# Channel mix moved to a matrix product, x by key read from a host-laid copy, three-slot pipeline

## The chip, the cores and the metric

One Trainium2 chip, one of its cores. The metric is the device time of one execution in microseconds (us), lower is better. Engines are named as in the profile: PE is TensorE (matmuls; PEld its weight loads), ACT is ScalarE, DVE is VectorE, POOL is GpSimd, and SP is SyncE, which issues the DMAs.

## The reference

x is 16 images of 256 channels and 64 x 32 pixels, float32 throughout. For each image (n is the pixel index, N = 2048):

```
alpha = relu(bn(wa @ x))           # 32 x N, queries
sigma = relu(bn(ws @ x))           # 32 x N, keys
att   = softmax over m of alpha[:, n] . sigma[:, m], only the 8 neighbours m of pixel n
h_s   = att @ x                    # spatial mix
Gc    = x x^T                      # 256 x 256, only channels c-1 and c+1 are used
catt  = softmax of Gc over the two neighbouring channels
h_p   = catt @ x                   # channel mix: two weights for each channel
out   = (1 - gama) * x + gama * elu(h_s + h_p)
```

## The kernel before

**Layout.** x of an image lies as 128 partitions by 2 halves: partition p holds channels 2p (h = 0) and 2p + 1 (h = 1), so that one neighbour of a channel is in the same partition and the other in a partition beside it. An image is cut into 4 quarters of 16 rows, 512 pixels. One quarter is a step s, 64 steps in all. Pixels are also cut into 16 groups of 128 keys; a query tile of 64 pixels needs a window of 128 keys.

**What a step computes.** `scores` (PE) writes masked windows of query by key to a bank of PSUM, two steps in one call (steps s and s + 1, for even s). `maxima` (DVE) adds the mask and takes the row maxima, `exp_scores` (ACT) exponentiates with row sums, `normalise` (DVE) divides and writes `probs`, `transpose_probs` (PE) turns it, `move_probs` copies it from PSUM to `probs_t`, and `z_sums` (PE) accumulates the spatial mix into the two banks z of the step, in two phases of 9 matmuls (`phase` 0 and 1, z_half between them). For the product PE needs x with keys on the partitions: that is `upper`, made by `transpose_x` (PE, 4 transposes of 128 x 128, two calls a step) and `move_xt` (ACT).

**The channel mix.** `weigh_own` (ACT) first writes 1 + catt * (the neighbour in the same partition) to z. `build_near` (SP) copies the other half of x one partition up or down into `near`, four DMAs a step, SBUF to SBUF. `mix_channels` (DVE) adds catt * near to z. Only then does `z_sums` accumulate on top. `exp_z` (ACT), `elu_out` (DVE), `keep_x` and `add_elu` (POOL) make the elu and the blend, and SP stores the result.

**Per image.** The projections `project_query`, `project_odd` (with two transposes of the image's last 64 keys, L525) and `project_even` fill a shared bank `gb` in turn, each waiting until ACT has emptied it (`move_query`, `move_odd`, `move_even`). `gram_band` (PE, 68 matmuls in four parts) makes the diagonals of Gc from `upper`; `gram_pick`, `shift_gram`, `gram_softmax_in`, `exp_gram` and `gram_softmax_out` turn them into `catt`.

**Order.** Each engine runs a loop over slots t, written by hand. In slot t the kernel works on scores and softmax of step t, on the transpose and the channel mix of step t - 1, on `z_sums` of step t - 2, on exp, elu and store of step t - 3, and on the transposes of x one image ahead. q is t modulo 4; the per-image work hangs on q. Engines meet only through counting semaphores. x has three buffers (XBUFS), `upper` and `near` two, `blend` four, z two pairs of banks, and the one bank `tr` takes both the turned x and the turned probabilities. Matmuls of float32 appear in the trace as two instructions each; transposes as one.

Nearly all matmuls are issued by the helper `mm`, so they have line 485, and the tiles written tell them apart: z from probs_t is `z_sums`, gb from x is a projection, gb from upper is the gram, score is the scores. Line 500 is `transpose_x`, line 581 `transpose_probs`.

## Time and profile before

| | us |
|---|---|
| median of 3 runs | 462.85 |
| lowest, highest | 458.08, 465.39 |
| the profiled execution | 457.33 |
| its span, first to last instruction | 455.5 |
| PE busy | 422.3 (93%) |
| DVE busy | 351.2 (77%) |
| ACT busy | 339.0 (74%) |
| POOL busy | 295.4 (65%) |
| DMA moved | 102.05 MB, mean 224 GB/s |

The profile describes the profiled execution alone. Its span leaves out 1.8 us that lie around the first and the last instruction. The span has three stretches: a start to about 38 us, in which the first image comes in and the pipeline fills; a repeating pattern of one image; and an end from about 424 us, in which the last image has no successor to prepare.

### The profile page before, as it was taken

To read this page: it belongs to the slowest core of one execution; us is meant where nothing else is said; L and a number is where in the kernel's file an instruction comes from. 1 tells how busy PE (TensorE), PEld (TensorE's weight loads), DVE (VectorE), ACT (ScalarE), POOL (GpSimd) and SP (SyncE) were. 2 spreads that over 40 slices of the span, in tenths; PEclk is the share of its full clock that TensorE was granted. 3 is DMA by queue.
4 is the path that set the end of the run, shared out by engine and by line. 5 is a ranking of instruction groups with operands and counts; after the bars stand their busy time and mean duration, and the time that the engine had idled before them with its cause. 6 is when DMAs were issued, how large, how long until landed. Compare 5 with 4: busy or idle time off the path is not lost.

```text
span 455.5 us, 18204 instructions
## 1 busy us (share of the span) xinstructions
PE 422.3 (93%) x7118; PEld 319.3 (70%) x7120; DVE 351.2 (77%) x1138; ACT 339.0 (74%) x980; POOL 295.4 (65%) x198
## 2 busy tenths in 40 slices
PE   6859999999999999999999989998999999999783
PEld 3426867677686777778676767877677786867673
DVE  1145878878887897888789778877978788888976
ACT  5447788686877978686888868687887868878651
POOL 5301676578588676858676676777667676787760
PEclk9959999999999999999999999999999999999776
DMA  7695678587777868777787877778687777855223
GB/s 223 187 250 155 200 253 250 195 264 229 234 246 243 265 224 264 243 229 234 246 270 222 250 232 228 243 239 268 190 263 246 228 251 237 257 183 191 96 85 148
DMA packets 55750, 102.05 MB, mean 224 GB/s; under 512 B 6256, under 2 KB 6640, under 8 KB 55664
## 3 DMA queue, kind: packets, MB, share of 16 engines
q1 hardware_dynamic: 55376, 100.81, 70.8%
q8 instruction: 57, 0.93, 0.9%
q14 instruction: 29, 0.24, 0.2%
q10 hardware_dynamic: 288, 0.07, 0.1%
HBM read 34.00 MB, written 33.55 MB: 148 GB/s over the span
## 4 chain that ended last, share of the span: by engine, by line
PE 71%; DVE 18%; issue 3%; DMA 3%; ACT 2%; SPq 1%; DVEq 0%; ACTq 0%
PE z L485 23%; PE gb L485 20%; PE tr L500 13%; PE score L485 7%; PE tr L581 6%; DVE elu L403 4%; DMA x<-x_dram 3%; DVE score L374 3%; DVE probs_t L391 2%; DVE probs L383 2%; PE gb L525 1%; DVE gb L418 1%; DVE band L414 1%; DVE neg_max L374 1%; DVE row_inv L379 1%
## 5 line engine op out<-in xcount | busy, mean ns | idle before, releaser
L485 PE MATMUL z<-probs_t,upper 64*128 64x128 f32 (+1 forms) x2304 | 173.7, 285 | 2.3 <-DVE z L398 1.2
L485 PEld LDWEIGHTS z<-probs_t,upper 64*128 64x128 f32 x2304 | 155.7, 191 | 22.0 <-issue 20.7
L239 POOL TENSOR_TENSOR blend<-elu,blend 128x1024 f32<-128x1024 f32 x61 | 144.1, 2363 | 9.4 <-POOL elu L235 0.5
L229 POOL TENSOR_SCALAR blend<-x,mix 128x1024 f32<-128x1024 f32 x64 | 71.8, 1123 | 98.8 <-DMA out_dram<-blend 98.7
L403 DVE SCALAR_TENSOR_TENSOR elu<-elu,z 128x512 f32<-128x512 f32 x128 | 82.1, 683 | 38.0 <-ACT elu L311 38.0
L288 ACT ACTIVATE score<-score,neg_max 128x128 f32<-128x128 f32 x256 | 86.7, 339 | 28.0 <-DVE neg_max L374 28.0
L311 ACT ACTIVATE elu<-z 128x512 f32<-128x512 f32 x128 | 69.7, 604 | 41.1 <-PE z L485 41.1
L261 ACT ACTIVATE upper<-tr 128x512 f32<-128x512 f32 x122 | 73.2, 600 | 34.7 <-PE tr L500 33.8
L235 POOL TENSOR_SCALAR elu<-elu,vec,mix 128x1024 f32<-128x1024 f32 x61 | 72.6, 1190 | 34.7 <-DVE elu L403 34.7
L398 DVE SCALAR_TENSOR_TENSOR z<-near,catt,z 128x512 f32<-128x512 f32 x128 | 89.9, 748 | 0.0
L500 PE MATMUL tr<-const,x 128*128 128x128 f32 x488 | 78.2, 283 | 11.4 <-DVE probs_t L391 7.2
L302 ACT ACTIVATE z<-x,catt 128x512 f32<-128x512 f32 x128 | 83.9, 697 | 2.3 <-DVE elu L403 2.3
L374 DVE CUSTOM_DVE_ANT_0 score<-score,const 128x128 f32<-128x128 f32 x256 | 66.7, 323 | 24.3 <-PE score L485 24.3
L500 PEld LDWEIGHTS tr<-const,x 128*128 128x128 f32 x488 | 53.4, 143 | 39.1 <-issue 34.3
L485 PE MATMUL gb<-x,wt 128*32 128x512 f32 (+2 forms) x720 | 65.7, 483 | 2.6 <-DMA x<-x_dram 2.6
L288 ACT ACTIVATION_READ_ACCUMULATOR score<-score,neg_max 128x1 f32 x256 | 53.1, 207 | 0.0
L383 DVE TENSOR_TENSOR probs<-score,row_inv 128x512 f32<-128x512 f32 x64 | 44.3, 692 | 2.2
L581 PE MATMUL tr<-const,probs 128*128 128x128 f32 x256 | 42.9, 291 | 2.7 <-DVE probs L383 1.9
L391 DVE COPY probs_t<-tr 128x512 f32<-128x512 f32 x64 | 44.0, 687 | 0.9 <-PE tr L581 0.9
L485 PE MATMUL score<-key,query 32*64 32x128 f32 x1024 | 36.2, 279 | 3.1 <-DVE probs L383 2.4
L485 PEld LDWEIGHTS gb<-x,wt 128*32 128x32 f32 x720 | 19.0, 110 | 25.4 <-issue 12.0
L374 DVE DVE_READ_ACCUMULATOR2_ANT neg_max<- 128x1 f32 x256 | 36.3, 142 | 0.0
(64 smaller groups left out, 254.1 us busy)
## 6 DMA issues: line engine op xcount, KB each, us to landing
x<-x_dram SPq DMA_DIRECT2D x64, 512.0 KB, 5.5
out_dram<-blend SPq DMA_DIRECT2D x61, 512.0 KB, 4.3
near<-x SPq DMA_DIRECT2D x128, 224.0 KB, 4.4
near<-x SPq DMA_DIRECT2D x128, 30.0 KB, 4.0
out_dram<-blend SPq DMA_DIRECT2D x6, 256.0 KB, 2.0
const<-constants_dram SPq DMA_DIRECT2D x1, 243.5 KB, 8.0
const<-constants_dram SPq DMA_DIRECT2D x1, 128.0 KB, 2.2
wt<-w_dram ACTq DMA_DIRECT2D x1, 64.0 KB, 2.8
```

What stands on the lines that cost most here:

```text
L229: nc.gpsimd.tensor_scalar(blend[s % BLENDS][:, :, :], xs[b % XBUFS][:, :, cols(q)], mix[:, 0:1], 0.0 if s < TAIL else mix[:, 1:2], ALU.mul ...
L235: nc.gpsimd.tensor_scalar(elu[s % 2][:, :, :], elu[s % 2][:, :, :], vec[:, V_GAMA:V_GAMA + 1], mix[:, 1:2], ALU.mult, ALU.add).then_inc(ga ...
L239: nc.gpsimd.tensor_tensor(blend[s % BLENDS][:, :, :], elu[s % 2][:, :, :], blend[s % BLENDS][:, :, :], ALU.add).then_inc(blend_done, 1)
L261: nc.scalar.activation(upper[b % 2][:, g:g + 2, :], xt_bank(b, q, i)[:, :].rearrange("p (v c) -> p v c", v=2), ACT.Copy).then_inc(xt_out, 1)
L288: last = nc.scalar.activation(at, at, ACT.Exp, bias=neg_max[s % 2][:, v:v + 1], scale=-1.0, accum_out=row_sum[s % 2][:, v:v + 1])
L302: nc.scalar.activation(z[s % 2][h][:, :], xs[b % XBUFS][:, 1 - h, cols(q)], ACT.Identity, scale=catt[:, h, 1 - h:2 - h], bias=1.0).then_in ...
L374: last = nc.vector.tensor_tensor_reduce(at, at, mask, -1.0, TOP, ALU.add, ALU.min, neg_max[s % 2][:, v:v + 1])
L398: nc.vector.scalar_tensor_tensor(zh[:, :], near[b % 2][:, h, q * QN:(q + 1) * QN], catt[:, h, h:h + 1], zh[:, :], ALU.mult, ALU.add).then_ ...
L403: nc.vector.scalar_tensor_tensor(elu[s % 2][:, h, :], elu[s % 2][:, h, :], 1.0, z[s % 2][h][:, :], ALU.min, ALU.max).then_inc(elu_done, 1)
L485: return nc.tensor.matmul(o, l, r, start=start, stop=stop, skip_group_check=True, **kw)
L500: last = nc.tensor.transpose(to[:, v * C + h * P:v * C + (h + 1) * P], xb[:, h, at0:at0 + WIN], ident)
L581: last = nc.tensor.transpose(tr[:, v * P:(v + 1) * P], probs[s % 2][:, v, :], ident)
```

## The change

- A second copy of x comes from the host, laid out by key: `x_t`, 16 x 128 x 17 x 256. SP loads it straight to `upper` (`load_upper`, two DMAs an image). `transpose_x`, `move_xt`, the two edge transposes of `project_odd` and their copy are gone. `upper` has three buffers.
- `near`, `build_near` and its four DMAs a step are gone. The channel mix is a matrix product: `build_diag` (DVE, four instructions an image) makes two 128 x 128 matrices with catt on two diagonals, `turn_diag` (PE) transposes them, `move_mixer` (ACT) copies them to `mixer`, and `mix_channels` (now on PE) multiplies them with x, two matmuls of 128 x 128 by 512 a step, accumulating to z.
- `weigh_own` becomes `set_one` (ACT): it writes 1 to z. `mix_channels` of DVE is gone. `move_probs` moves from DVE to ACT.
- The pipeline has three slots instead of four: in slot t, `transpose_probs`, `mix_channels`, both phases of `z_sums`, `exp_z` and `elu_out` all belong to step t - 1, and the store to t - 2. `gram_band` runs in one piece, an image ahead, and catt is ready an image ahead.
- `scores` of the next two steps stand at the end of the odd slots.

The loops that set the order, on PE, ACT and DVE, and the new helpers:

```
-            for t in range(STEPS + 3):
+            for t in range(STEPS + 1):
                 b, q = t // QUARTERS, t % QUARTERS
-                if b + 1 < B:
-                    transpose_x(b + 1, q, 0)
...
+                ahead = b + 1 < B
+                if real(t - 1):
                     transpose_probs(t - 1)
+                    mix_channels(t - 1)
+                if q == 1 and ahead:
+                    shift_gram(b + 1)
+                if q == 2 and ahead:
+                    project_query(b + 1)
+                if q == 3 and ahead:
+                    project_even(b + 1)
+                if real(t - 1):
+                    z_sums(t - 1, 0)
+                    z_sums(t - 1, 1)
+                if q == 0 and b < B:
+                    turn_diag(b)
+                if q == 0 and ahead:
+                    gram_band(b + 1)
+                if q == 2 and ahead:
                     project_odd(b + 1)
+                if q % 2 == 1 and t + 1 < STEPS:
+                    scores(t + 1)
```

```
+            def mix_channels(s):
+                b, q = s // QUARTERS, s % QUARTERS
+                pe.wait_ge(mixer_out, b + 1)
+                for h in range(HALF):
+                    pe.wait_ge(one_done, 2 * s + h + 1)
+                    mm(z[s % 2][h][:, :], mixer[:, h * P:(h + 1) * P], xs[b % XBUFS][:, 1 - h, cols(q)], False, True)
...
             def project_even(b):
                 xb = xs[b % XBUFS]
                 if b > 0:
-                    pe.wait_ge(odd_out, 2 * (b + 1))
+                    pe.wait_ge(odd_out, b + 1)
...
+            def turn_diag(b):
+                pe.wait_ge(diag_done, b + 1)
+                if b > 0:
+                    pe.wait_ge(pt_out, b * QUARTERS)
+                for h in range(HALF):
+                    last = nc.tensor.transpose(tr[:, h * P:(h + 1) * P], diag[:, h, :], ident)
+                last.then_inc(mixer_done, 1)
```

ACT, the new slot:

```
+                if real(t - 1):
+                    move_probs(t - 1)
+                for h in range(HALF):
+                    if real(t):
+                        set_one(t, h)
+                if q == 3 and ahead:
+                    move_odd(b + 1)
+                if real(t):
+                    exp_scores(t)
+                if q == 1 and ahead:
+                    exp_gram(b + 1)
+                if q == 2 and ahead:
                     move_query(b + 1)
+                if q == 3 and ahead:
+                    move_even(b + 1)
                 for h in range(HALF):
                     if real(t - 1):
+                        exp_z(t - 1, h)
+                if q == 0 and b < B:
+                    move_mixer(b)
```

DVE, the new slot:

```
+                if q == 1 and ahead:
+                    gram_pick(b + 1)
                 if real(t):
                     maxima(t)
+                if q == 1 and ahead:
+                    gram_softmax_in(b + 1)
+                if real(t):
                     normalise(t)
+                if q == 1 and ahead:
+                    gram_softmax_out(b + 1)
+                if q == 3 and ahead:
+                    build_diag(b + 1)
                 for h in range(HALF):
                     if real(t - 1):
+                        elu_out(t - 1, h)
```

SP at the start, and the load of `upper`:

```
+            def load_upper(b, i):
+                if b >= XBUFS:
+                    sp.wait_ge(z_done, (b - XBUFS) * QUARTERS + 2 * i + 2)
+                g = slice(i * GROUPS // 2, (i + 1) * GROUPS // 2 + i)
+                sp.dma_start(upper[b % XBUFS][:, g, :], x_t[b][:, g, :]).then_inc(upper_in[b % XBUFS][i], 16)
...
+            for q in range(QUARTERS):
                 load_x(0, q)
+            sp.dma_start(const[:, :], constants).then_inc(masks_in, 16)
+            for i in range(2):
+                load_upper(0, i)
+            sp.wait_ge(query_done, 1)
+            for i in range(2):
+                load_upper(1, i)
+            sp.wait_ge(score_done, 2)
+            for q in range(QUARTERS):
+                load_x(1, q)
```

PE in the kernel before, slots q = 2 and q = 3 of an image (score is for the next two steps, tr from probs is `transpose_probs`, tr from x is `transpose_x`, gb from x and wt a projection; the two gb rows are project_odd and project_even, z from probs_t is one phase of `z_sums` in three rows):

```order
L485 MATMUL score<-key,query 64x128 x16
L581 MATMUL tr<-const,probs 128x128 x4
...
L485 MATMUL gb<-x,wt 32x256 x8
L525 MATMUL gb<-const,x 64x128 x2
L500 MATMUL tr<-const,x 128x128 x4
...
L500 MATMUL tr<-const,x 128x128 x4
...
L581 MATMUL tr<-const,probs 128x128 x4
L485 MATMUL gb<-x,wt 32x320 x8
L500 MATMUL tr<-const,x 128x128 x4
```

PE in the changed kernel, from project_odd at the end of slot q = 2 to the end of slot q = 3 (z from x and mixer is the new `mix_channels`):

```order
L462 MATMUL gb<-x,wt 32x256 x8
L550 MATMUL tr<-const,probs 128x128 x4
L462 MATMUL z<-x,mixer 128x512 x2
L462 MATMUL gb<-x,wt 32x320 x8
L462 MATMUL z<-probs_t,upper 128x64
L462 MATMUL z<-probs_t,upper 128x128 x7
L462 MATMUL z<-probs_t,upper 128x64 x2
L462 MATMUL z<-probs_t,upper 128x128 x7
L462 MATMUL z<-probs_t,upper 128x64
L462 MATMUL score<-key,query 64x128 x16
```

Between project_odd and project_even there were a transpose group of x, both `z_sums` phases and more; now there is one `transpose_probs` and one `mix_channels`. The two phases of `z_sums` follow each other with nothing between.

ACT in the kernel before, around the copy of project_odd (L272) in slot q = 3, to the copy of project_even (L281):

```order
L261 ACTIVATE upper<-tr 128x512
L272 ACTIVATE key<-gb,bn 128x256
L276 ACTIVATE upper<-gb 64x256
L302 ACTIVATE z<-x,catt 128x512 x2
L288 ACTIVATE score,row_sum<-score,neg_max 128x128 x4
L261 ACTIVATE upper<-tr 128x512
L281 ACTIVATE key<-gb,bn 128x320
```

ACT in the changed kernel, slot q = 3 (L278 is `move_probs`, L285 `set_one`, L251 `move_odd`, L263 `exp_scores`, L256 `move_even`, L291 `exp_z`):

```order
L278 ACTIVATE probs_t<-tr 128x512
L285 ACTIVATE z<-zeros_b 128x512 x2
L251 ACTIVATE key<-gb,bn 128x256
L263 ACTIVATE score,row_sum<-score,neg_max 128x128 x4
L256 ACTIVATE key<-gb,bn 128x320
L291 ACTIVATE elu<-z 128x512 x2
```

The copy of project_odd now stands behind `move_probs` and the two `set_one` of its slot.

## Rows read from the trace of the kernel before

**Rows 1.** The page: busy time, and by 40 slices the granted clock and GB/s.

```profile
PE 422.3 (93%) x7118; PEld 319.3 (70%) x7120; DVE 351.2 (77%) x1138; ACT 339.0 (74%) x980; POOL 295.4 (65%) x198
...
PEclk9959999999999999999999999999999999999776
...
GB/s 223 187 250 155 200 253 250 195 264 229 234 246 243 265 224 264 243 229 234 246 270 222 250 232 228 243 239 268 190 263 246 228 251 237 257 183 191 96 85 148
```

**Rows 2.** Chain that ended last, one image: start us, us, what.

```profile
203.32 0.63 PE tr L500 x4
...
208.68 1.25 PE z L485 x18
...
209.94 0.39 PE gb L485 x32
210.33 0.59 PE tr L500 x4
...
220.18 1.03 PE score L485 x32
221.21 0.59 PE tr L581 x4
...
224.05 0.34 PE gb L525 x2
...
229.74 0.63 PE tr L500 x4
```

**Rows 3.** Stretches: us, PE, PEld, DVE, ACT, POOL busy (instructions), granted clock, DMA share, GB/s.

```profile
24.00:32.00 8.00, 3.08 (x16) 1.98 (x20) 5.39 (x22) 4.37 (x14) 0.00 (x0) 0.55 1.00 260
200.00:226.40 26.40, 25.72 (x447) 19.57 (x445) 21.73 (x70) 20.90 (x62) 17.64 (x13) 1.00 0.78 243
420.00:440.00 20.00, 17.42 (x245) 15.57 (x244) 16.35 (x56) 11.55 (x38) 14.43 (x10) 0.74 0.24 90
```

**Rows 4.** Timeline, weight loads of the first projection, four beside each other.

```profile
12.81 0.13 PEld L485 LDWEIGHTS z<-x,wt 128*32 128x32 f32 x4 [0.30 <-issue]
13.24 0.13 PEld L485 LDWEIGHTS z<-x,wt 128*32 128x32 f32 x4 [0.30 <-issue]
13.67 0.13 PEld L485 LDWEIGHTS z<-x,wt 128*32 128x32 f32 x4 [0.30 <-issue]
```

**Rows 5.** Timeline, weight loads of both z_sums phases of one step, back to back.

```profile
442.39 1.19 PEld L485 LDWEIGHTS z<-probs_t,upper 64*128 64x128 f32 x18 [0.17 <-issue]
443.77 1.19 PEld L485 LDWEIGHTS z<-probs_t,upper 64*128 64x128 f32 x18 [0.20 <-PE z L485]
```

**Rows 6.** Groups by form: shapes, count, busy us, mean ns, idle before, releaser.

```profile
L311 ACT ACTIVATE elu<-z 128x512 f32<-128x512 f32 x128 | 69.7, 604 | 41.1 <-PE z L485 41.1
...
L374 DVE CUSTOM_DVE_ANT_0 score<-score,const 128x128 f32<-128x128 f32 x256 | 66.7, 323 | 24.3 <-PE score L485 24.3
L288 ACT ACTIVATION_READ_ACCUMULATOR score<-score,neg_max 128x1 f32 x256 | 53.1, 207 | 0.0
L383 DVE TENSOR_TENSOR probs<-score,row_inv 128x512 f32<-128x512 f32 x64 | 44.3, 692 | 2.2
...
L485 PE MATMUL gb<-x,wt 128*32 128x512 f32 x240 | 30.4, 626 | 2.6 <-DMA x<-x_dram 2.6
...
L272 ACT ACTIVATE key<-gb,bn 128x256 f32<-128x256 f32 x15 | 8.7, 579 | 0.0
```

**Rows 7.** Timeline: four score exponentials of one step, start to start, on ACT.

```profile
203.09 0.33 ACT L288 ACTIVATE score<-score,neg_max 128x128 f32<-128x128 f32 x1
...
203.43 0.33 ACT L288 ACTIVATE score<-score,neg_max 128x128 f32<-128x128 f32 x1
```

**Rows 8.** Timeline, start: last quarter of image 0 lands; first turned probabilities.

```profile
11.33 0.66 PE L500 MATMUL score<-const,x 128*128 128x128 f32 x4 [0.19 <-DMA x<-x_dram]
...
26.23 1.09 PE L581 MATMUL tr<-const,probs 128*128 128x128 f32 x4 [0.88 <-ACT upper L261]
```

**Rows 9.** Timeline, end: exp of the last step, once its z_sums are done.

```profile
449.80 1.09 ACT L311 ACTIVATE elu<-z 128x512 f32<-128x512 f32 x2 [3.58 <-PE z L485]
```

More of the change, by code:

```diff
@@ L27 @@
 EVEN, ODD = 5 * KEYS, 4 * KEYS
-EDGE = ODD
-SPREAD = 112
-NEARS = 4 * 16
-C_ID, C_DOWN = 0, P
-C_BAND = 2 * P
+C_ID, C_DOWN, C_UP = 0, P, 2 * P
+C_BAND = 3 * P
 C_END = C_BAND + 3 * BAND
@@ L37, with graph_attention @@
 C_ALL = C_MASK + 3 * WIN
-TAIL = STEPS - 3
+TAIL = STEPS - 2
 V_GAMA = 8
-def graph_attention(nc, x, w_t, vectors, constants, out):
+def graph_attention(nc, x, x_t, w_t, vectors, constants, out):
     fp32, bf16 = mybir.dt.float32, mybir.dt.bfloat16
@@ L65, in graph_attention @@
         xs = [sb(f"x{j}", [P, HALF, N + 4 * W]) for j in range(XBUFS)]
-        near = [sb(f"near{j}", [P, HALF, N]) for j in range(2)]
-        upper = [sb(f"upper{j}", [P, GROUPS + 1, C]) for j in range(2)]
+        upper = [sb(f"upper{j}", [P, GROUPS + 1, C]) for j in range(XBUFS)]
         const = sb("const", [P, C_ALL])
@@ L154, in graph_attention @@
         ident = const[:, C_ID:C_ID + P]
-        slots = range(-QUARTERS, STEPS + 3)
         def real(s):
@@ L245, in _ @@
             pool.wait_ge(bn_done, 1)
-            for j in range(2):
-                nc.gpsimd.memset(near[j][:, :, :], 0.0).then_inc(near_zero, 1)
-            for t in slots:
-                if real(t - 1):
-                    keep_x(t - 1)
-                if 0 <= t - 3 < TAIL:
-                    add_elu(t - 3)
+            for t in range(STEPS + 1):
+                if real(t):
+                    keep_x(t)
+                if 0 <= t - 1 < TAIL:
+                    add_elu(t - 1)
         @block.scalar
         def _(act):
-            def move_xt(b, q, i):
-                g = GQ * q + 2 * i
-                act.wait_ge(xt_done, 2 * QUARTERS * b + 2 * q + i + 1)
-                if b >= 2:
-                    act.wait_ge(z_done, (b - 2) * QUARTERS + q + 1)
-                nc.scalar.activation(upper[b % 2][:, g:g + 2, :],
-                                     xt_bank(b, q, i)[:, :].rearrange("p (v c) -> p v c", v=2), ACT.Copy).then_inc(xt_out, 1)
             def move_query(b):
@@ L293, in exp_gram, with move_mixer, move_probs, set_one @@
                 nc.scalar.activation(powers, gram_d[:, :, :], ACT.Exp).then_inc(gram_exp, 1)
-            def weigh_own(s, h):
-                b, q = s // QUARTERS, s % QUARTERS
-                act.wait_ge(catt_done, b + 1)
+            def move_mixer(b):
+                act.wait_ge(mixer_done, b + 1)
+                nc.scalar.activation(mixer[:, :], tr[:, 0:HALF * P], ACT.Copy).then_inc(mixer_out, 1)
+            def move_probs(s):
+                act.wait_ge(pt_done, s + 1)
+                if s >= 2:
+                    act.wait_ge(z_done, s - 1)
+                nc.scalar.activation(probs_t[s % 2][:, :], tr[:, :], ACT.Copy).then_inc(pt_out, 1)
+            def set_one(s, h):
                 if s < 2:
@@ L318, in _ @@
             nc.scalar.activation(warm[:, :], bn[:, 0, 0:1], ACT.Exp)
-            for q in range(QUARTERS):
-                for i in range(2):
-                    move_xt(0, q, i)
             act.wait_ge(bn_done, 1)
@@ L437, in gram_softmax_out, with build_diag @@
                                         ALU.mult).then_inc(catt_done, 1)
+            def build_diag(b):
+                dve.wait_ge(catt_done, b + 1)
+                if b > 0:
+                    dve.wait_ge(mixer_done, b)
+                for h in range(HALF):
+                    step = nc.vector.tensor_scalar(diag[:, h, :], ident, catt[:, h, 1 - h:2 - h], None, ALU.mult)
+                    if h == HALF - 1:
+                        then(step)
+                for h, at in enumerate((C_DOWN, C_UP)):
+                    last = nc.vector.scalar_tensor_tensor(diag[:, h, :], const[:, at:at + P], catt[:, h, h:h + 1],
+                                                          diag[:, h, :], ALU.mult, ALU.add)
+                last.then_inc(diag_done, 1)
             nc.vector.memset(zeros_b[:, :], 0.0).then_inc(zeros_done, 1)
@@ new lines, in _ @@
+            gram_band(0)
+            pe.wait_ge(query_out, 1)
+            pe.wait_ge(odd_out, 1)
+            for i in range(2):
+                for h in range(HALF):
+                    last = mm(z[i][h][:, :], zeros_b[:, 0:P], zeros_b[:, :], True, True)
+            last.then_inc(z_open, 1)
+            pe.wait_ge(masks_in, 16)
+            shift_gram(0)
+            for t in range(STEPS + 1):
+                b, q = t // QUARTERS, t % QUARTERS
+                ahead = b + 1 < B
+                if real(t - 1):
+                    transpose_probs(t - 1)
+                    mix_channels(t - 1)
[13 more added lines that the diff above has]
+                if q == 2 and ahead:
+                    project_odd(b + 1)
+                if q % 2 == 1 and t + 1 < STEPS:
+                    scores(t + 1)
```

247 lines of the change are left out of this document (63 added, 184 removed).

## The prediction

> **What bounds the kernel now.** I read the page first, then the chain that ended last, then the stretches, then single blocks in the timeline. The page has PE at 93% with every other engine at 77% or less [rows 1]. That figure is modelled, so it is checked in the chain: there one image, from one transpose group of x to the same group of the next image, takes 229.74 - 203.32 = 26.4 us, and nearly every piece of it is a PE block that starts when the one before has gone in [rows 2]. The stretch of the same length has PE busy for 25.7 of 26.4 us at a granted clock of 1.00, that is at its upper level, and the DMA engines at 0.78 with 243 GB/s [rows 3]. So in the repeating part PE's own instruction stream sets the time, about 0.6 us an image apart, and 16 images at 26.4 us are 422 of the 455.5 us. What ACT, DVE and POOL shed is worth nothing there; what PE gains or sheds counts in full.
>
> **What PE sheds.** Eight transpose groups of x an image, 0.59 to 0.63 us from start to start [rows 2]: 8 x 0.61 = 4.9 us. The two edge transposes are 0.34 us [rows 2]. Sum 5.2 us an image.
>
> **What PE takes on.**
> - The channel mix: two products of 512 columns a step, each two instructions in float32, so four instructions one behind the other. The trace has no full-width product of this length. The nearest is the first projection, also 512 columns: its groups of four instructions, which lie beside each other in four column strips, start 0.43 us apart (12.81, 13.24, 13.67) [rows 4]. The transposes are not far off, 4 x 128 columns in 0.59 us with a gap behind them [rows 2]. One strip or the whole width streams the same columns, so an instruction takes 0.43 us and a step 4 x 0.43 = 1.71 us. The low end is 1.7 us. The high end takes the mean of one instruction, 626 ns [rows 6], for the last of each half, as if its end were exposed: 1.71 + 2 x 0.2 = 2.1 us. I take 1.8, near the starts, since matmuls here overlap: 7.2 us an image.
> - Two transposes of diag, at half a group of four, with a gap: 0.35 us an image. Bounds 0.3 and 0.6.
> - The two z_sums phases were always kept apart by other work. Back to back they exist once or twice at the end: 442.39 to 443.77 is 1.38 us [rows 5], against 1.25 us for a phase with something else behind it [rows 2]. Phase 1 waits for phase 0 to land. 0.13 x 4 = 0.5 us an image.
> - A new wait. In slot q = 3 project_even stands behind transpose_probs (0.59) and the mix (1.8) and needs the copy of project_odd, which ACT makes after move_probs and two set_one. Those are 512-column ACT operations of the 604 ns kind, 0.54 to 0.6 us apart [rows 6]. With S for PE's start of the slot: the turned probabilities are there at S + 0.7, move_probs ends at S + 1.35, the two ones at S + 2.6, the copy (579 ns [rows 6]) at S + 3.2. PE arrives at S + 2.4, so it stands 0.9 us, with both z_sums phases, the scores and the whole slot queued behind it. Bounds: nothing, if ACT gets to move_odd early, and 1.5 us.
>
> So an image takes 26.4 - 0.5 (the idle time in it, mostly waits around tr and the gram that go) - 5.2 + 7.2 + 0.35 + 0.5 + 0.9 = 29.65, say 29.6 us. The mix alone is 2 us dearer than all that is removed.
>
> **What lies beside it.** Does the shorter pipeline hold? From the slot's start S: ones written S + 2.6; exp_scores, four at 0.34 from start to start plus the last accumulator read of 0.2 [rows 6, 7], to S + 4.15; reciprocal and normalise, 692 ns [rows 6], to S + 5.05. The next transpose_probs wants it at S + 6 or later, since the shortest slot with extras (q = 1) is 0.59 + 1.8 + 2.63 + 1.03 = 6.05 us. elu and the next maxima (323 ns kind [rows 6], at most 1.3 us for four) end at S + 2.4 of the next slot, before the ones do. move_probs (S + 1.35) is covered by the mix to S + 2.4. The diag work on DVE, four short operations, stands ahead of elu_out where DVE waits for z_sums anyway. ACT gives up move_xt and takes move_probs, DVE gives up mix_channels: both cost nothing, because PE covers them, and neither gives anything. If the cover failed by x us in a slot it would cost 64x. Loads: near's SBUF traffic goes and 2.23 MB of x_t an image come, 2.1 + 2.1 + 2.2 = 6.4 MB an image, which is 217 GB/s at 29.6 us. The trace reached 243 at a share of 0.78 and 260 at 1.00 [rows 3]. So it fits.
>
> **Start, last image, end.** PE cannot go past gram_band(1) before x(0), the constants and upper of images 0 and 1 have landed: 2.1 + 0.45 + 2 x 2.23 = 7.0 MB. At 243 GB/s [rows 3] and 2 us for the first bytes that is 30.8 us; before, 2.2 MB were in at 11.33 us [rows 8]. The catt chain on DVE (gram, softmax, diag, maxima, normalise) ends at about the same time. gram_band, 136 instructions at 0.39 us for 32 [rows 2], is 1.7 us. PE is nearly idle from about 24 us on; in the kernel before, such a stretch had a granted clock of 0.55, and a transpose group then took 1.09 us instead of 0.66 [rows 3, 8], so I add 1 us: slot 1 starts at 33.5 us, with the mix and z_sums of step 0 still to come (before, that step's z_sums began near 38 us, but with a later image further prepared). Then the rest of image 0: 29.6 - 7.1 = 22.5 us. Images 1 to 14: 14 x 29.6 = 414.4 us. Image 15 has hardly any extras, and a slot there is set by the loop of elu, maxima, exp and normalise at some 6.0 us: 24 us, and the last slot 5 us. The end from the last z_sums on stays: 449.8 to 455.5 [rows 9], 5.7 us. Sum: 33.5 + 22.5 + 414.4 + 29 + 5.7 = 505.1 us of span, 506.9 us with the 1.8 us around it, against 457.3 us for the execution profiled: +10.8%. That execution lies 1.2% under the median of the runs shown, so the median may come out some us higher; the clock penalty and the wait of 0.9 us are more likely too high than too low. I forecast 506 us.
>
> **Rivals.**
> - *Not slower: the product streams faster than the projection does.* The one number that makes the sum is 1.8 us a step. If a full-width product with preloaded weights went at 0.26 us an instruction, a step would pay 1.05 us, 0.75 less, 48 us over 64 steps: 458 us, no change. It decides below about 1.1 us a step. Against it: three starts at 0.43 us with weights loaded well ahead [rows 4]. Chance 0.04. The Trainium skill, "TensorE: Matmul & The Clock Gate", section "Back-to-back issue gap", gives 131 ns a matmul of 512 columns as the sustained spacing with pipelining and 216 ns isolated; by that ratio 0.43 would become 0.26. This trace does not agree, its back-to-back starts keep 0.43 us.
> - *The loads become the bound.* If stores, x and the long rows of x_t reach only 200 GB/s together, an image takes 6.4 MB / 200 = 32 us, and 14 images more cost 14 x 2.4 = 34 us: 540 us. For it: all loads and stores stand in SP's one queue, and single slices of the page go as low as 155 to 200 GB/s [rows 1]. Against: 243 GB/s with 0.22 to spare [rows 3], and the small DMAs of near go. It decides under 217 GB/s. Chance 0.08.
> - *The shorter pipeline becomes the bound.* exp_z, elu, maxima, exp_scores and normalise now follow each other within two slots; with 0.2 us of hand-over more at each of six steps, normalise would end at S + 6.3 in the short slots and later in the fuller ones, and a slot would take about 7.8 us: 64 x 0.4 = 26 us more, 532 us. For it: ACT waits 41.1 us for z_sums and DVE 24.3 us for scores even before [rows 6]. Against: 1 us of slack in the shortest slot by the sum above. Chance 0.12.
> - *PE runs at its stream alone.* No wait at project_even, a head without loss: 16 x 0.9 + 3 = 17 us less, 489 us. Chance 0.12.
>
> **How the numbers follow.** The forecast has 0.64, its own range 496 to 518 (product 1.7 to 2.1 us a step, the low side at once with a smaller wait). 489 us and part of the two dear cases belong in the range: 484 to 528. A measurement of this kernel tells about 2% from no change. Slower by over 2%, that is over 472 us: all but the first rival, 0.95. Within 2%: 0.04. Faster: 0.01.
>
> **What would show it.** In the changed profile: mix instructions on PE starting 0.43 us apart and some 110 us of PE time for them; PE busy 93% or more; one image 29 to 30 us apart; a PE wait for ACT's key copy, some 15 times and near 0.9 us; both z_sums phases 1.38 us apart; ACT and DVE idle longer than before; first probs transposed after 31 us. Wrong would be: starts of 0.26 us; PE waiting for DVE's probs or for x_t in most slots; an image under 27 us.

## The result and the profile after

| | before | changed |
|---|---|---|
| median of 4 runs, us | 462.68 | 497.69 |
| lowest, highest | 458.08, 465.39 | 496.14, 499.42 |
| ratio to before, 95% interval | | 1.079 (1.070 to 1.088) |
| span of the profiled execution | 455.5 | 494.3 |

The change makes the kernel 8% slower. The forecast was 506 us in a range of 484 to 528: right in direction and range, 8 us too high. Where executions of a kernel lay more than 1.5% above its fastest one, ratios leave them out.

The page of the changed kernel, first part, then granted clock and GB/s in 40 slices; it answers to [rows 1]:

```profile
PE 459.3 (93%) x6867; PEld 306.3 (62%) x6868; DVE 260.2 (53%) x1008; ACT 302.0 (61%) x916; POOL 291.4 (59%) x198
...
PEclk9759999999999999999999999999999999999998
...
GB/s 265 366 226 240 204 218 205 230 237 229 251 207 201 217 227 245 233 251 204 224 189 230 243 235 240 217 218 201 233 232 238 243 210 218 183 81 51 86 87 129
```

PE is still at 93% of a longer span. DVE has shed 91 us and ACT 37 us, and both only wait longer: ACT's exp_z now stands 105.5 us for z_sums, 41.1 before [rows 6]. The largest groups of the new work and of the waits, by line:

```profile
L291 ACT ACTIVATE elu<-z 128x512 f32<-128x512 f32 x128 | 69.5, 594 | 105.5 <-PE z L462 105.5
...
L462 PE MATMUL z<-x,mixer 128*128 128x512 f32 x256 | 121.6, 598 | 0.0
```

The product keeps PE busy 121.6 us (its modelled ends overlap what follows), against 78.2 us for the transposes of x and 6.1 us for the edge that have gone. The chain that ended last, one image of it (start us, us, what), answers to [rows 2]:

```profile
201.68 0.59 PE tr L550 x4
...
206.62 0.37 PE tr L524 x2
206.99 1.61 PE gb L462 x130
...
214.70 0.59 PE tr L550 x4
215.28 1.72 PE z L462 x4
...
218.86 1.27 PE z L462 x18
220.13 0.04 issue
220.17 1.32 PE z L462 x18
...
223.12 0.60 ACT probs_t L278
223.72 1.01 ACT z L285 x2
224.73 0.49 ACT key L251
...
225.26 1.28 PE gb L462 x16
...
230.22 0.58 PE tr L550 x4
```

The reader is to see four things. The image takes 230.22 - 201.68 = 28.5 us (28.8 on average over images 1 to 14), against 26.4. The product, four instructions, takes 1.72 us. The phases of z_sums follow each other at 1.31 us (218.86 to 220.17), then 1.32 us to the next block. And the chain leaves PE once an image, for ACT: turned probabilities, two ones, the key copy, and only then project_even. That wait shows on PE as 0.46 us a time (rows of waits: us in total, times, longest). The second row, issue, is time in which PE stands still and the profile shows nothing that it waits for; the text calls this a stop:

```profile
PE gb L462 <- ACT key L251: 6.9, 15, 0.5
...
PE gb L462 <- issue: 6.5, 6, 3.4
```

### The profile page after: what moved, and what is told of

Read it like the earlier page. It is cut to its first block, busy times and chain, and to the rows that moved or that the text cites. A ratio compares the mean times of both kernels' runs of the same rounds, so it can differ in the third digit from the quotient of the medians.

```text
span 494.3 us, 16718 instructions
## 1 busy us (share of the span) xinstructions
PE 459.3 (93%) x6867; PEld 306.3 (62%) x6868; DVE 260.2 (53%) x1008; ACT 302.0 (61%) x916; POOL 291.4 (59%) x198
## 4 chain that ended last, share of the span: by engine, by line
PE 86%; ACT 7%; issue 3%; DMA 2%; DVE 2%; SPq 0%; ACTq 0%
PE z L462 52%; PE gb L462 18%; PE tr L550 8%; PE score L462 7%; ACT z L285 3%; ACT probs_t L278 2%; DMA x<-x_dram 2%; ACT key L251 1%; PE tr L524 1%; SPq L165 0%; ACT elu L291 0%; DVE z L367 0%; ACT score L263 0%; DVE elu L367 0%; DVE blend L373 0%
## 5 line engine op out<-in xcount | busy, mean ns | idle before, releaser
L462 PEld LDWEIGHTS z<-probs_t,upper 64*128 64x128 f32 x2304 | 152.2, 187 | 47.7 <-issue 34.0
L462 PE MATMUL z<-probs_t,upper 64*128 64x128 f32 (+1 forms) x2304 | 170.1, 280 | 3.7
L229 POOL TENSOR_TENSOR blend<-elu,blend 128x1024 f32<-128x1024 f32 x62 | 146.1, 2357 | 9.5 <-POOL elu L225 0.4
L291 ACT ACTIVATE elu<-z 128x512 f32<-128x512 f32 x128 | 69.5, 594 | 105.5 <-PE z L462 105.5
L367 DVE SCALAR_TENSOR_TENSOR elu<-elu,z 128x512 f32<-128x512 f32 x124 | 79.7, 684 | 80.2 <-ACT elu L291 80.2
L462 PE MATMUL z<-x,mixer 128*128 128x512 f32 x256 | 121.6, 598 | 0.0
L263 ACT ACTIVATE score<-score,neg_max 128x128 f32<-128x128 f32 x256 | 87.5, 343 | 2.2 <-DVE neg_max L351 2.2
L285 ACT ACTIVATE z<-zeros_b 128x512 f32<-128x512 bf16 x128 | 71.2, 594 | 0.0
L462 PE MATMUL gb<-x,wt 128*32 128x512 f32 (+2 forms) x720 | 64.2, 474 | 6.9 <-ACT key L251 6.9
L278 ACT ACTIVATE probs_t<-tr 128x512 f32<-128x512 f32 x64 | 38.2, 597 | 47.4 <-PE tr L550 47.3
L356 DVE RECIPROCAL row_inv<-row_sum 128x4 f32<-128x4 f32 x64 | 11.4, 178 | 101.0 <-ACT score L263 101.0
L462 PEld LDWEIGHTS z<-x,mixer 128*128 128x128 f32 x256 | 44.2, 193 | 31.2 <-issue 31.2
L263 ACT ACTIVATION_READ_ACCUMULATOR score<-score,neg_max 128x1 f32 x256 | 53.9, 210 | 0.0
L550 PEld LDWEIGHTS tr<-const,probs 128*128 128x128 f32 x256 | 27.1, 142 | 16.0 <-issue 14.6
```

What stands on the lines that cost most here:

```text
L229: nc.gpsimd.tensor_tensor(blend[s % BLENDS][:, :, :], elu[s % 2][:, :, :], blend[s % BLENDS][:, :, :], ALU.add).then_inc(blend_done, 1)
L263: last = nc.scalar.activation(at, at, ACT.Exp, bias=neg_max[s % 2][:, v:v + 1], scale=-1.0, accum_out=row_sum[s % 2][:, v:v + 1])
L278: nc.scalar.activation(probs_t[s % 2][:, :], tr[:, :], ACT.Copy).then_inc(pt_out, 1)
L285: nc.scalar.activation(z[s % 2][h][:, :], zeros_b[:, :], ACT.Identity, bias=1.0).then_inc(one_done, 1)
L291: nc.scalar.activation(elu[s % 2][:, h, :], z[s % 2][h][:, :], ACT.Exp, bias=-1.0)\
L367: nc.vector.scalar_tensor_tensor(to, elu[s % 2][:, h, :], 1.0, z[s % 2][h][:, :], ALU.min, ALU.max).then_inc(elu_done, 1)
```

## The experiments

Each row of times is the median; the kernel before, run beside them, had 462 to 463.4 us.

**Doubling the product (e3).** It leaves the channel mix counted twice.

```
                     mm(z[s % 2][h][:, :], mixer[:, h * P:(h + 1) * P], xs[b % XBUFS][:, 1 - h, cols(q)], False, True)
+                    mm(z[s % 2][h][:, :], mixer[:, h * P:(h + 1) * P], xs[b % XBUFS][:, 1 - h, cols(q)], False, True)
```

> Changed kernel with each product of mixer and x issued twice; it leaves the channel mix counted twice. Theory: 4 more instructions of 0.43 us a step, all on the path: + 64 x 1.72 = +110 us, 607 us, minus up to 7 us since the wait of PE for ACT's key copy is covered. Rival (the product is partly hidden): clearly under +110 us.

Measured: 600.42 us, one run, +102.7 us. With the 6.9 us of the key wait that the longer product covers, that is 109.6 / 64 = 1.71 us a step. In its chain the doubled product is 3.44 us:

```profile
218.99 3.44 PE z L462 x8
```

So added PE work of this kind costs its full streaming time. This confirms that the product is a full term of the sum.

**Taking the key wait away (e1).**

```
+                if q == 3 and ahead:
+                    move_odd(b + 1)
                 for h in range(HALF):
                     if real(t):
                         set_one(t, h)
-                if q == 3 and ahead:
-                    move_odd(b + 1)
```

> Changed kernel with one move on ACT: the copy of project_odd goes ahead of the two set_one of its slot. Theory (PE's own stream sets the time, and what PE waits counts in full): the waits of PE for ACT's key copy, 0.46 us fifteen times, are gone and an image is 0.46 us shorter, 7 us in all: about 491 us, no new wait of PE in their place. Rival (the ACT and DVE loop sets the time, PE only follows it): set_one and the exponentials are 0.5 us later in that slot, so nothing is gained, 497 us, or PE waits for probs instead.

Measured: 490.9 us (490.06 to 491.67), ratio 1.065 (1.055 to 1.075), 6.8 us less than the changed kernel. Its chain in slot q = 3 is PE alone, product and project_even back to back:

```profile
220.63 0.59 PE tr L550 x4
221.22 1.72 PE z L462 x4
222.94 1.22 PE gb L462 x16
```

So what PE waits here counts, and about 7 of the 35 us that the change costs are an order of instructions on ACT. The match of 6.8 us with the 6.9 us waited is closer than these runs can tell: the two profiled executions differ by 5.2 us of span, and e1's has 12.0 us of stops against 7.8 us.

**Breaking up the two phases of z_sums (e5, e5b).**

```
-                    mix_channels(t - 1)
+                    mix_channels(t - 1, 0)
...
                     z_sums(t - 1, 0)
+                    mix_channels(t - 1, 1)
                     z_sums(t - 1, 1)
```

> Changed kernel in which the product of half 0 stays ahead of the z_sums phases and that of half 1 goes between phase 0 and phase 1 (slot q = 3 keeps project_even ahead of phase 0). Theory: the wait of phase 1 for phase 0 (0.04 us and the 1.32 us instead of 1.25 us up to the next block) goes, 0.1 us a step, 6 us in all: about 491 us; the copy of the turned probabilities (0.6 us on ACT) is still covered by one product of 0.86 us and the transposes. Rival: that cover is too short, PE waits 0.1 to 0.3 us for probs_t in the slots with nothing else ahead of z_sums and the time is 497 us or more.

Measured: 512.49 us (511.59 to 513.22), 14.8 us slower than the changed kernel. (z_sums also waits for both ones before phase 0, since half 1 is now multiplied behind it.) The theory was wrong on both counts; the rival, a cover too short and 497 us or more, had the direction. Phase, product and phase take 3.57 us where the pieces apart are 1.31 + 0.86 + 1.32 = 3.49, so no gap was saved:

```profile
223.78 3.57 PE z L462 x38
```

And the half product that moved away had been cover: the wait for the key copy, which the rival did not name, grew from 6.9 to 19.8 us, 12.9 of the 14.8 us. The weight loads of phase 0 now wait for the turned probabilities, up to 1.0 us a time, which is more than the 0.1 to 0.3 us named:

```profile
PE gb L462 <- ACT key L251: 19.8, 15, 1.3
...
PEld z L462 <- ACT probs_t L278: 14.7, 19, 1.0
```

The second edit adds e1's order to it.

> Both edits at once: the copy of project_odd ahead of set_one (491 us alone) and the second product between the z_sums phases. Theory (both are pieces of PE's own stream and add up): 497.7 - 6.8 - 6 = 485 us. Rival (one loop of ACT and DVE takes over): no more than the better of the two.

Measured: 497.55 us (494.22 to 498.04). e1's order takes 15 us off, since it brings the larger wait down from 19.8 to 4.2 us. The sum is no better than the changed kernel, and 6.6 us worse than e1 alone: the rival's number. No loop of ACT and DVE is needed for it: the split costs 0.08 us a step (3.57 against 3.49), 5 us in all, and 4.2 us of the key wait are left.

**Doubling the loads by key (e4).** A second load into a buffer that nobody reads, 31 MB in all.

```
                 sp.dma_start(upper[b % XBUFS][:, g, :], x_t[b][:, g, :]).then_inc(upper_in[b % XBUFS][i], 16)
+                if b >= 2:
+                    if b > 2:
+                        sp.wait_ge(spare_in[i], 16 * (b - 2))
+                    sp.dma_start(spare[:, g, :], x_t[b][:, g, :]).then_inc(spare_in[i], 16)
```

> Changed kernel in which every load of x by key from image 2 on is done twice, the second time to a spare buffer that nobody reads: 31 MB more. Theory (the loads are far from the bound: 104 MB at a DMA share of 0.65): share goes to about 0.8, time stays within 5 us of 497 us. Rival (the loads or the one queue of SP already set part of the time): 515 us or more, with PE waiting for x or upper.

Measured: 510.86 us (508.99 to 512.73, two runs), +13 us, between the two expectations, with a DMA share of 73% in place of 62%. After the start PE does not wait for x or upper. What has grown is idle time of PE for which the profile shows no releaser. The waits of PE in this kernel, and then the same lines of the changed kernel (the third had 6.5, 1.0 and 0.3):

```profile
PE gb L470 <- issue: 14.0, 9, 3.2
PE tr L558 <- issue: 3.0, 1, 3.0
PE z L470 <- issue: 1.0, 1, 1.0
```

18.0 us against 7.8 us: 10 of the 16.6 us by which the spans of the two profiled executions differ. Most stand in the gram, 68 matmuls that go in as 272 short instructions (136 loads, 136 matmuls) in 1.6 us.

Where the stops stand says more than their sum. Before the eleven stops over 0.35 us of e4, PE had recorded 444, 697, 2461, 3215, 4979, 6743, 7497, 8505, 9261, 11024 and 11779 instructions, weight loads and matmuls together. The distances are 1, 7, 3, 7, 7, 3, 4, 3, 7 and 3 times 252. The changed kernel has six such stops, behind 444, 696, 2460, 4978, 6742 and 11023 instructions: six of the same places. Behind the first two, where the second load has not begun, PE stood 3.41 and 1.07 us in the changed kernel and 2.82 and 1.34 us in e4; at the other four 0.98, 0.39, 0.45 and 1.00 us became 3.19, 1.22, 2.73 and 2.98 us. One caution: e1, with the loads of the changed kernel, stood 1.46, 2.45, 1.21 and 0.98 us at these four, so a part of the growth is chance.

**Leaving the product out (e2).** The channel mix is left out.

```
                 for h in range(HALF):
                     pe.wait_ge(one_done, 2 * s + h + 1)
-                    mm(z[s % 2][h][:, :], mixer[:, h * P:(h + 1) * P], xs[b % XBUFS][:, 1 - h, cols(q)], False, True)
```

> Changed kernel without the two products of mixer and x on PE; it leaves out the channel mix, all waits and all other instructions stay. Theory: PE's stream sheds 4 x 0.43 us a step, 110 us; an image would be 28.7 - 6.9 = 21.8 us by PE alone, but then the loop over transpose, copy of the probabilities, z_sums, exp, elu, maxima, exponentials and normalise (some 5.5 to 6 us a slot) takes over for the short slots, so 405 to 425 us, with waits of PE for ACT's probs_t and DVE's probs. Rival (the product lies beside something and costs little): over 470 us. Rival (PE alone): 388 us.

Measured: 478.24 us (475.90 to 480.58, two runs), only 19 us less, where 110 us of PE instructions are gone. The theory and the rival of PE alone missed; the other rival (over 470 us) was right in its number for a wrong reason, as e3 shows: the product hides behind nothing. The page, then PE's waits, and what one group of PE costs now:

```profile
PE 382.5 (80%) x6612; PEld 289.4 (60%) x6612; DVE 256.3 (54%) x1008; ACT 300.3 (63%) x916; POOL 291.3 (61%) x198
...
PEclk9959999989999996699999898998989899899655
```

```profile
PE gb L462 <- ACT key L251: 34.0, 15, 2.3
...
PE z L462 <- ACT probs_t L278: 17.3, 21, 0.9
...
PE score L462 <- DVE probs L360: 10.5, 14, 0.8
```

```profile
L462 PE MATMUL z<-probs_t,upper 64*128 64x128 f32 (+1 forms) x2304 | 192.1, 305 | 21.0 <-ACT probs_t L278 17.3
```

Two things came up. The waits for ACT and DVE, 7 us with the product, are 67 us without it (the three rows and 5.1 us for DVE's gram); the product had covered them. And the granted clock, 1.00 in the stretches of the changed kernel's repeating part, drops in many slices: 0.90 over the span, where the changed kernel has 0.98. The same instructions then take longer: z_sums 192.1 us in place of 170.1, the projections 69.8 in place of 64.2, scores and transposes 3.7 us more, 31 us together. 110 - 60 - 31 leaves 19 us, which is what was measured (15.5 us between the two spans).

**Without the product and without the key wait (e9).** The product's line is gone as in e2, and the copy of project_even on ACT goes behind exp_z.

```
+                if q == 3 and ahead:
+                    move_odd(b + 1)
                 for h in range(HALF):
                     if real(t):
                         set_one(t, h)
...
                     z_sums(t - 1, 0)
                     z_sums(t - 1, 1)
+                if q == 3 and ahead:
+                    project_even(b + 1)
```

> The kernel without the product (478 us, 21 to 22 us an image by PE's instructions alone, 27 measured) with its largest new wait taken out too: project_even goes behind z_sums in slot q = 3 and its copy behind exp_z, and the copy of project_odd goes ahead of set_one. It leaves out the channel mix. Theory (without the product PE is no longer the bound by itself but stands in a loop with ACT and DVE, and the 34 us that it waited for ACT's key copy were on the path): 445 to 450 us. Rival (the clock sets it: granted 0.90 because PE idles, whatever it waits for): no more than 10 us gained, over 468 us.

Measured: 475.38 us (471.69 and 479.06), 3 us less than e2, inside the spread of both; the faster execution alone is 6.55 us below e2's median. The theory of the loop alone (445 to 450 us) falls, and the rival, at most 10 us gained and over 468 us, holds in its number. The largest wait is gone, and its time came back elsewhere: the wait for probs_t grew from 17.3 to 30.4 us, and 11.8 us for the even key copy are new. A stretch of the chain of the 479.06 us execution shows what the clock does, and below it stands one stretch with the columns of [rows 3]:

```profile
250.28 0.66 PE gb L462 x56
250.94 2.21 issue
253.16 1.03 PE gb L462 x67
...
255.66 2.33 PE z L462 x18
```

```profile
254.20:258.00 3.80, 3.41 (x24) 2.99 (x24) 2.27 (x16) 3.10 (x12) 2.57 (x2) 0.57 0.59 199
```

PE stops for 2.21 us in the gram, goes on for 1.03 us and waits again for 0.9 us, and the phase of z_sums behind that takes 2.33 us where it took 1.31 us just before. The granted clock was 1.00 up to 254.2 us and is 0.57 in the stretch shown: it has gone to its lower level.

**Zeros in the product's place (e12).** On top of e9; the channel mix is left out.

```
                     pe.wait_ge(one_done, 2 * s + h + 1)
+                    for _ in range(2):
+                        mm(z[s % 2][h][:, :], zeros_b[:, 0:P], zeros_b[:, :], False, True)
```

> The kernel without the product and without the key wait (475 us, granted clock 0.90) with four bfloat16 products of zeros, 512 columns each, added in every step where the product of mixer and x stood (it leaves out the channel mix; the zeros add nothing). That is 0.85 us more work for PE in a step at the upper clock, 55 us in all. Theory (most of what leaving the product out should have given is given back by the clock, which falls when PE pauses): the granted clock returns to 0.96 or more, the waits for probs_t are covered, and an image is some 25.3 us: 445 us, faster than with less work. Rival (PE's stream or the loop of ACT and DVE simply adds): the zeros cost up to 55 us: 475 to 530 us.

Measured: 463.6 us (461.01 to 467.29, ten runs), ratio 1.006 (1.002 to 1.011): with 256 matmuls more, 0.86 us a step and 55 us in all, it is 8 us faster than the faster execution of e9 and 12 us faster than the mean of the two. PE's wait for probs_t (30.4 us in e9) is gone, and the granted clock is 0.965. The same z_sums, projections, scores and transposes take 29 us less than in e9's profile (z_sums 170.9 us in place of 189.0). So the waits filled and the clock regained are of like size. The page's clock, and then the largest wait of PE:

```profile
PEclk8759999999999989999899999999999899999999
```

```profile
PE gb L462 <- issue: 14.5, 9, 3.4
```

So keeping PE busy gave back more than the zeros cost, but the theory had asked for 30 us: the clock is not the whole. The stops in the gram are still there, 14.5 us, and PE still waits for the even key copy (11.8 us) and for probs (5.5 us).

**One part alone: loads by key in the kernel before (e8).** The transposes, their copies and waits go; x_t is loaded as in the change; the neighbour copies and the mix stay.

```
+            def load_upper(b, i):
+                if b >= XBUFS:
+                    sp.wait_ge(z_done, (b - XBUFS) * QUARTERS + 2 * i + 2)
...
-                if b + 1 < B:
-                    transpose_x(b + 1, q, 0)
...
-                if b + 1 < B:
-                    move_xt(b + 1, q, 0)
```

> The kernel before with one part of the change alone: x by key loaded from the host-laid copy, three upper buffers, no transposes of x on PE, no copies of them on ACT, no edge transposes; neighbour copies, the mix on ACT and DVE and the four slots stay. Theory (PE's stream): 5.2 us an image shed, 16 images, at most 83 us: 380 us if nothing else bound. It will not come to that: DVE needs 5.5 us a step, 351 us, and all DMAs together 136 MB with the small rows of near, about 415 us at a share of 1.00: 420 to 440 us. Rival (only the DMAs count now): 462 us or more. Either way this part by itself is expected faster than the kernel before.

Measured: 455.04 us (452.65 and 457.43), ratio 0.983 (0.974 to 0.992). Faster than before, but by 8 us, where the theory had 420 to 440 us; the rival (only the DMAs count, 462 us or more) missed too. The DMAs are busy nearly throughout; the page with the shares of its chain, and then one stretch with the columns of [rows 3]:

```profile
DMA  7999999999999999999999999999999999966233
...
q1 hardware_dynamic: 59984, 136.46, 93.9%
...
PE 45%; DVE 32%; issue 12%; DMA 4%; ACT 3%; SPq 3%; POOL 1%; DVEq 0%; ACTq 0%
```

```profile
196.00:244.00 48.00, 42.70 (x815) 33.17 (x814) 40.24 (x128) 32.51 (x98) 33.78 (x22) 0.96 1.03 331
```

That the loads are the bound is not shown by this. After the start no engine waits for x, near or upper. The chain goes through PE and DVE, which is busy for 40 of the 48 us; PE's stops are 33.6 us, against 4.0 us before, and the granted clock over the span is 0.896, against 0.969, with z_sums at 189.6 us in place of 173.7. PE sheds some 83 us here; how much of it went to the stops, to the clock and to the loop with DVE was not isolated.

**The mix on ACT and DVE in the changed kernel (e7).** The product, diag and mixer go; the neighbour channels come from a third host-laid copy; scores move behind transpose_probs, project_odd to slot q = 3.

```
-                nc.scalar.activation(z[s % 2][h][:, :], zeros_b[:, :], ACT.Identity, bias=1.0).then_inc(one_done, 1)
+                nc.scalar.activation(z[s % 2][h][:, :], xs[b % XBUFS][:, 1 - h, cols(q)], ACT.Identity,
+                                     scale=catts[b % 2][:, h, 1 - h:2 - h], bias=1.0).then_inc(product_done, 1)
...
+                nc.vector.scalar_tensor_tensor(zh[:, :], near[b % 2][:, h, q * QN:(q + 1) * QN], catts[b % 2][:, h, h:h + 1],
+                                               zh[:, :], ALU.mult, ALU.add).then_inc(mix_done, 1)
...
+                sp.dma_start(near[b % 2][:, :, c], x_n[b][:, :, c]).then_inc(near_in[b % 2][i], 16)
```

> The changed kernel's loads by key and its three slots, but the channel mix back on ACT and DVE as before, its neighbour channels read from a third host-laid copy (34 MB more, rows of 4 KB); scores after transpose_probs in even slots, project_odd and project_even both in slot q = 3. Theory (PE's stream counts, and the product is what makes the change slow): PE sheds the product and the diag work, 7.2 us an image, and the waits seen when only the product was left out are avoided by the order: 22.5 to 24 us an image, 410 to 430 us, faster than both. Rival (the loads): 138 MB at the 340 GB/s that a share of 1.00 would carry is 405 us if perfect, more likely 450 us and above with PE waiting for near or upper. Rival (clock): PE is idle a quarter of the time, its granted clock falls in stretches and the time stays above 450 us.

Measured: 454.05 us (452.23 to 455.20), ratio 0.981 (0.976 to 0.986). It beats both kernels, 9 us ahead of before and 44 us ahead of the changed one, but is 24 us short of the expectation. Both rivals had named 450 us and above. That of the loads expected PE to wait for near or upper, and it does not; that of the clock fits better, at 0.877 over the span, with z_sums at 189.2 us in place of 170.1. The page's granted clock, then a piece of the chain with a stop of PE within transpose_probs, then the stretches before and behind the stop (columns of [rows 3]):

```profile
PEclk9756999779598999999598899979859689999995
```

```profile
211.33 0.48 PE tr L538 x3
211.80 3.24 issue
215.05 0.48 PE tr L538
...
216.20 2.40 PE z L460 x18
218.65 2.39 PE z L460 x18
```

```profile
200.00:211.80 11.80, 11.37 (x283) 8.61 (x280) 9.85 (x30) 10.37 (x30) 9.79 (x7) 1.00 0.99 365
...
216.20:221.00 4.80, 4.74 (x37) 4.44 (x37) 2.84 (x8) 2.63 (x11) 0.79 (x1) 0.50 1.04 403
```

This stop, too, stands a whole number of 252 instructions behind the first: 6494 recorded, against 444 + 24 x 252 = 6492, though the order of the program is another one.

**Two attempts to better it (e10, e11).** The first spreads the gram and takes shift_gram, project_query and the gram softmax off the path:

```
+                if q == 0 and ahead:
+                    gram_band(b + 1, 0)
...
                     z_sums(t - 1, 1)
                 if q == 0 and ahead:
-                    gram_band(b + 1)
+                    gram_band(b + 1, 1)
+                if q == 1 and ahead:
+                    shift_gram(b + 1)
+                if q == 2 and ahead:
+                    project_query(b + 1)
```

> The version with the mix on ACT and DVE, neighbours and keys from host-laid copies (454 us), with the order mended: shift_gram and project_query behind z_sums, the gram in two pieces ahead of and behind z_sums, the gram softmax behind the elu on DVE. Theory (PE waits of 7 us for the gram, 1.5 us for catt and part of 15.5 us without a releaser behind the gram's 272 short instructions are on the path): 435 to 445 us. Rival (the loads, with 138 MB, hold the pipeline up wherever it is): 450 us or more.

The second puts zeros ahead of transpose_probs:

```
+                    pe.wait_ge(mix_done, 2 * t)
+                    for _ in range(3):
+                        mm(z[(t - 1) % 2][0][:, :], zeros_b[:, 0:P], zeros_b[:, :], False, True)
                     transpose_probs(t - 1)
```

> The version with the mix on ACT and DVE and neighbours from a host-laid copy (454 us, granted clock 0.88) with three bfloat16 products of zeros of 512 columns ahead of each transpose_probs, where PE waits for DVE. They add 0.64 us of PE work a step, 41 us. Theory (the clock's fall is what keeps this version at 454 us): granted clock 0.95 or more and 430 to 440 us. Rival (the loads, 138 MB, hold it): 454 us or more, PE waits without a releaser as long as before.

Measured: 479.7 us for e10 (466.57 to 495.12; the two fastest of six 466.57 and 471.94) and 481.63 us for e11 (476.05 to 487.88; the four fastest up to 481.9). Both theories were wrong by more than 20 us, e11's by more than 35 us, and both rivals (450 us or more, 454 us or more) hold in their numbers.

In e10 PE's wait for DVE's gram went as planned (7.1 us), but the wait for catt stayed at 1.5 us, and the waits for probs_t grew from 3.3 to 12.4 us and for the query copy from 0 to 3.9 us. The stops in the gram rose from 15.5 to 26.3 us, but all stops only from 25.7 to 28.2 us. The granted clock in the profiled execution (480.07 us) is 0.84, against 0.877 in e7; yet the execution of 466.57 us has 0.878 and is still 11 us above e7's slowest, so the clock explains only a part.

In e11 the clock rose only to 0.91. The stops are 33.3 us (23.7 us in gb), more than e7's 25.7, and the zeros' 41 us were paid on top. How stops, waits and clock share the loss was not isolated.

## Why the prediction was right, and where it was off

- *PE's stream bounds the kernel; what is added to it counts in full.* Shown: the chain, and e3 (1.71 us a step for a doubled product), e1 (6.8 us for a 6.9 us wait, within the noise told there).
- *The product, 1.8 us a step.* Measured 1.72, the low end of the stated bounds: the ends of the two halves are not exposed. 14 x 4 x 0.08 = 4.5 us of the error.
- *The new wait, 0.9 us an image, and its place.* Right place, 15 times, but 0.46 us: move_probs ends 1.22 us into the slot (223.72 - 222.50), not 1.35, the two ones take 1.01 us, not 1.25, and the copy releases after 0.49 of its 0.56 us. 14 x 0.44 = 6.2 us of the error. The prediction had called this term likely too high.
- *The phases back to back 0.5 us an image, the diag transposes 0.35 us.* Measured 1.31 us from phase to phase, not the 1.38 named, and 1.32 us behind: with 1.25 us for a phase by itself that is 0.13 us a step all the same. The diag transposes are 0.37 us. Both terms right.
- *The image, 29.6 us.* Measured 28.8: these two terms (product and wait) are nearly all of the 0.8 us.
- *The head, slot 1 at 33.5 us.* The first transpose_probs began at 34.14 us, but what set it was not what the sum had. The sum lets the loads, 7.0 MB, run until 30.8 us. They moved 330 to 401 GB/s between 12 and 28 us, not 243, so the 7.0 MB were in before 24 us, and from 28 us on the DMAs were nearly idle (first row, columns of [rows 3]). In their place came what the sum did not add: stops of 3.41 and 1.07 us in the first two grams, and a wait of 2.7 us for DVE's diag, behind a chain over gram, softmax and diag from 25.4 to 29.9 us that the sum had let run beside the loads. That the head came out within 1 us is luck. The clock was at its lower level, as in its row: 1.11 us for the four.

```profile
28.00:32.00 4.00, 2.04 (x106) 1.71 (x109) 2.60 (x15) 2.23 (x10) 0.00 (x0) 0.50 0.21 79
...
34.14 1.11 PE L550 MATMUL tr<-const,probs 128*128 128x128 f32 x4
```

- *The end.* The slots of image 15 were 6.6, 6.0, 4.9 and 5.6 us against 6.0 forecast, and from the last z_sums on 6.0 us against 5.7.
- *A term not in the sum: PE's stops.* 4.0 us before, 7.8 us in the changed kernel; 4.5 of these are in the head.
- *The rivals.* A product at 0.26 us an instruction: no, 0.43 in the trace and in e3. The ratio in the Trainium skill ("TensorE: Matmul & The Clock Gate", section "Back-to-back issue gap") is not borne out here, nor is its 131 ns a matmul: e12's four bfloat16 products of 512 columns, one behind the other, take 0.86 us, 0.215 us each. The loads as the bound: not in this kernel, at 211 GB/s and a share of 62%, though e4 shows that 31 MB more already cost 13 us. The shorter pipeline as the bound: no, PE waited for probs once, 0.6 us. No run takes the pipeline or the transposes of x out of the changed kernel alone.
- *One sentence was wrong although the number came out: "what PE gains or sheds counts in full".* Only the first half holds. Of the 110 us that PE sheds in e2, 19 us became time. The product had covered waits for ACT and DVE and held the clock up. In e8 the kernel before sheds 83 us and gains 8. The forecast survived because the change added to PE in the sum. Had it shed 30 us net, the same reasoning would have promised nearly 30 us, and by e2 and e8 only a fraction might have come.

What makes the stops was not isolated, but the traces narrow it. Their places follow the count of PE's instructions in steps of 252 (250 in e9, e12 and the kernel before), whichever instruction stands there, a gram matmul, a z_sums matmul or one in the middle of a group of transposes, so a wait for a semaphore does not explain them. They show above all in the gram, where many short instructions go in within 1.6 us. They grow when the loads grow and PE's instructions stay (e4). That PE gets its instructions in blocks, and late where it uses them up fast and the DMAs are busy, would fit all of this; no run here shows it by itself.

## What to carry to other kernels

Work moved to the engine that bounds costs its stream: count it start to start, here 0.43 us for each of two instructions of a float32 product of 512 columns, and compare it with what leaves the same engine; relief of engines that wait anyway buys nothing. The reverse does not hold: before promising what removed work gives, list what it had covered, because the waits under it and the clock take most of it back. Add up the loads too, and read the stops and the clock that come with them: two changes that each cut PE (e8, e7) met at 138 MB and 454 to 455 us, with stops of 33.6 and 25.7 us and granted clocks of 0.90 and 0.88.

## What the runs showed of the hardware that was not expected

- PE with more work can be faster: four products of zeros a step took the kernel without the product from 472 to 479 us down to 464 us, and the granted clock from 0.90 to 0.965. The Trainium skill ("TensorE: Matmul & The Clock Gate", section "HAM oscillation — how this bites in real kernels") warns of pauses that bring the clock down; the traces agree, a phase of z_sums taking 2.33 us instead of 1.31 behind stops of 2.21 and 0.9 us, and 2.40 us instead of 1.27 behind one of 3.24 us.
- Loads with rows of 4 to 9 KB moved far more than the 243 to 260 GB/s seen before: the changed kernel itself reaches 401 GB/s between 12 and 16 us, when upper comes in, and e7 has slices of 401 to 426 GB/s through its whole length. e8, with its small rows, is at a share of 1.03 with 331 GB/s.
- PE's stops stand at fixed places, a multiple of 250 to 252 recorded instructions apart, in kernels of different order. They add up to 4.0 us before, 7.8 in the changed kernel, 18.0 with the doubled loads, 25.7 in e7 and 33.6 in e8; at the same loads as the changed kernel, e1 has 12.0 and e9 17.6 us.
